# Corner additions of the gathered tiles: on TensorE in every stage but the context stage

## The reference, cut to what matters

```python
x = x + _L0_conv_ref(_gn(x), ...)   # focal modulation: projections, three depthwise convolutions, gating
x = x + _L1_conv_ref(_gn(x), ...)   # layer norm and a quantised gated MLP
x = x + _L2_conv_ref(_gn(x), ...)   # 7x7 convolutions by FFT, gates, scan, projection
x = x + _L3_conv_ref(_gn(x), ...)   # deformable convolution:

offsets = conv3x3(x, offset_w) + offset_b          # 2 numbers for each of 9 taps
py, px = pixel + tap + offsets;  y0, x0 = floor(py), floor(px);  wy, wx = py - y0, px - x0
val = gather(y0, x0)     * ((1 - wy) * (1 - wx)) + gather(y0, x0 + 1)     * ((1 - wy) * wx) \
    + gather(y0 + 1, x0) * (wy * (1 - wx))       + gather(y0 + 1, x0 + 1) * (wy * wx)
out = einsum('bhwkc,kcf->bhwf', val, kernel) + bias
```

## Time and profile before

| | |
|---|---|
| median of 3 runs | 5363.71 us (5361.05 to 5369.22) |
| profiled execution, its own time | 5375.03 us |
| its span, first to last instruction | 5373.1 us |
| mean granted clock of PE | 0.675 of full speed |
| PE busy | 3023.5 us (56%) |
| DVE busy | 3301.6 us (61%) |
| POOL busy | 2852.9 us (53%) |
| ACT busy | 1723.2 us (32%) |

### The profile page before, as it was taken

One profiled execution on the slowest core, in us unless ns is written; L12 is line 12 of the kernel. 1 busy time (PEld: TensorE's weight loads), 2 busy tenths in 40 slices (PEclk: granted clock), 3 DMA queues, 4 the chain that ended last, 5 costly groups with the idle time before them and its releaser, 6 DMA issues. The chain is left out here.

```text
span 5373.1 us, 93043 instructions
## 1 busy us (share of the span) xinstructions
PE 3023.5 (56%) x39604; PEld 2643.3 (49%) x39604; DVE 3301.6 (61%) x4084; ACT 1723.2 (32%) x3209; POOL 2852.9 (53%) x2614
## 2 busy tenths in 40 slices
PE   2873235669644466569644466579744563554333
PEld 2872135559533355469533365469633453543222
DVE  4357843575678755675688666666779655454333
ACT  1223424721333235522234246422333242240000
POOL 1000000365566655665565666665666766777776
PEclk9965655569767666759666676769666755665555
DMA  6541174568633575658523566659433657554333
GB/s 165 121 83 23 29 137 129 151 141 190 137 92 106 123 195 165 177 131 194 135 80 108 148 169 183 163 138 208 126 98 97 164 165 179 174 164 124 103 105 93
DMA packets 776762, 727.31 MB, mean 135 GB/s; under 512 B 575244, under 2 KB 677036, under 8 KB 771916
## 3 DMA queue, kind: packets, MB, share of 16 engines
q1 hardware_dynamic: 651931, 381.46, 30.9%
q0 software_dynamic: 124416, 339.90, 21.9%
HBM read 601.34 MB, written 136.73 MB: 137 GB/s over the span
## 5 line engine op out<-in xcount | busy, mean ns | idle before, releaser
L2146 POOL DMA_INDIRECT e_gb<-corner_table,e_idx x2592 | 2838.3, 1095 | 2500.8 <-DMA e_cws<-cw_all 1043.8
L2208 DVE TENSOR_TENSOR e_vw<-e_gb,e_pc 128x1024 f32<-128x1024 f32 x576 | 773.0, 1369 | 692.7 <-DMA e_gb<-corner_table,e_idx 671.8
L2174 PE MATMUL e_pv<-shifts,e_vw 128*128 128x128 f32 x2768 | 557.5, 373 | 390.8 <-DVE e_vw L2215 390.8
L2174 PEld LDWEIGHTS e_pv<-shifts,e_vw 128*128 128x128 f32 x2768 | 461.1, 195 | 424.6 <-DVE e_vw L2215 401.8
L488 PE MATMUL e_pw<-wk,e_vt 128*64 128x64 f32 (+1 forms) x2880 | 333.7, 290 | 447.2 <-DVE e_xr L2226 236.6
L488 PEld LDWEIGHTS e_pw<-wk,e_vt 128*64 128x64 f32 (+1 forms) x2880 | 287.1, 197 | 512.0 <-issue 269.8
L2184 ACT ACTIVATE e_vt<-e_pv 128x512 f32<-128x512 f32 x288 | 182.4, 633 | 791.8 <-PE e_pw L2174 783.3
L502 PE MATMUL b_p<-b_x,b_tt 100*100 100x96 f32 x4096 | 375.6, 251 | 2.0 <-ACT b_x L815 2.0
L502 PEld LDWEIGHTS b_p<-b_x,b_tt 100*100 100x100 f32 x4096 | 370.3, 169 | 2.4 <-issue 1.6
L489 PE MATMUL e_pw<-wk,e_vt 128*64 128x64 f32 (+1 forms) x2880 | 335.0, 291 | 0.0
L2215 DVE TENSOR_TENSOR e_vw<-e_vw 128x1152 f32<-128x1152 f32 x230 | 322.5, 1402 | 7.9
(11 more groups left out here) (310 smaller groups left out, 7125.6 us busy)
## 6 DMA issues: line engine op xcount, KB each, us to landing
e_gb<-corner_table,e_idx POOLq DMA_INDIRECT x2592
d_px<-x_halo SPq DMA_DIRECT2D x32, 1152.0 KB
corner_table<-f_xn SPq DMA_DIRECT2D x128, 288.0 KB
b_tt<-zl_copies SPq DMA_DIRECT2D x128, 273.0 KB
b_tt<-zl_copies SPq DMA_DIRECT2D x128, 195.0 KB
f_xall<-xpad SPq DMA_DIRECT2D x10, 2400.0 KB
x_halo<-d_xo SPq DMA_DIRECT2D x128, 144.0 KB
d_wd<-wd_rows SPq DMA_DIRECT2D x8, 1890.0 KB
```

The costliest lines, as they stand in the source:

```text
L2146: nc.gpsimd.indirect_dma_start(self.gb[k][:, 4 * q:4 * q + 4, :].rearrange("p a c -> p (a c)"), None, T.table[m], off)\
L2174: last = nc.tensor.matmul(dst, vw[:, a, 2 * q:2 * q + nq, :].rearrange("p k c -> p (k c)"), T.ident[:, :], start=(a == 0), stop=(a == n - ...
L2208: v.tensor_tensor(dst, self.gb[k][:, 4 * k0:4 * k1, :].rearrange("p (k a) c -> p k a c", a=4), bc(w, [128, k1 - k0, 4, C], 3), ALU.mult).t ...
```

## The change

One condition in `plan()` differs. A tile joins `whole` when it is placed in any stage but B, instead of in L alone.

```diff
@@ -2328,7 +2328,7 @@
         while tiles < J * loaded and due <= clock:
-            if s == 3:
+            if s != 1:
                 whole.add(tiles)
             tile(tiles)
             due += spaces[(tiles - 1) // (NI * J)]
```

## The result

The changed kernel takes 5334.44 us (median of 7 runs, 5320.75 to 5343.37) against 5366.17 for the one before, timed in the same rounds: a ratio of 0.9936, 95% interval 0.9925 to 0.9948, which is 34 us less (28 to 40). The forecast was no change. The time lies inside the stated range, but the likeliest case was wrong: the kernel is faster, by 0.6%, and that is clear of the noise.

A forecast was written before the change was run, and what follows sets the result against it. It took POOL's gathers to bound the last part and a chain changing engines before it. Transposes 51, additions -53, clock -15, neighbouring paths +13, turns joining the chain +4 summed to 0: 5364 us, range 5330 to 5398.

The forecast's parts named there:

- the likeliest case: Whole kernel: added transposes and dropped additions cancel, 5364 us, its own range 5353 to 5374, chance 0.37.
- What bounds the kernel.: POOL issuing 72 tiles' gathers paces the last 895.5 us; before that the chain changes engine every few us.
- Nearly all of their work is hidden by POOL's gathers.: POOL's part, 33 changed tiles: gathers cover nearly all of their work; priced at -2 to +4 us.
- 53 us at most: Additions dropped from DVE: 42 on the chain at 1.27 us each save 53 us at most, nothing at least.
- the quarter taken off it as lost: Where an addition leaves the chain, a neighbouring path may be nearly as long: 13 us of the saving lost.
- The count: Chain from 3133 to 4477 runs through 18 additions, so 40 over all three rounds before POOL's part.
- 37 sets at 1.39 us: Ten more transposes per changed tile on PE: 37 sets on the chain cost 51 us, ends 40 and 79.
- The credit: Longer bursts leave PE at the full clock for longer: 0.4 us a set, 37 sets, 15 us gained.
- the last rival: Transposes on PE don't raise the clock, every added ten cost 2.13 us: +43 us, 5407, chance 0.08.
- The copies' rival: ACT's copies wait for PE's turns, mainly in D and F, wait up over 60 us: +33, 5397, chance 0.21.
- The faster rival: Bursts carry PE's clock, all 53 us realised, turns cost 40, credit 22: -35 us, 5329, chance 0.34.

The follow-up runs named there:

- late33: Kernel before, with only the 33 changed tiles from tile 216 on switched to twenty transposes and no addition: ratio 0.9963, -20 us.
- early_psum: Kernel before, in 116 of the 130 changed tiles before tile 216 the addition replaced by a same-size DVE instruction with second input from PSUM: 0.9981, -10 us.
- tail39: Kernel before, with only the 39 last tiles, after all stages, switched to twenty transposes and no addition: ratio 0.9971, -16 us.
- pe_early: Kernel before, additions kept, twenty transposes with ten thrown away in only the 130 changed tiles before tile 216: ratio 1.0052, +28 us.
- pe_half: Kernel before, additions kept, twenty transposes with ten thrown away in all 163 changed tiles: ratio 1.0064, +34 us.
- dve_half: Kernel before, additions dropped in the 163 changed tiles without the ten more transposes, corners 2 and 3 left out: ratio 0.9857, -77 us.
- df: Kernel before, with only the 78 changed tiles before tile 216 in stages D and F switched: ratio 0.9991, -5 us.
- tail_sbuf: Changed kernel, 39 last tiles switched too, plus a DVE dummy with both inputs in SBUF in 34 of them: 0.9958, -23 us against the kernel before.
- tail_psum: Changed kernel, 39 last tiles switched too, plus a DVE dummy with second input from PSUM in 34 of them: 0.9912, -47 us against the kernel before.

## Why the prediction was wrong, step by step

**What bounds the kernel.** Right: POOL paces the part behind the last group's first gather, and before it the chain changes hands. That was the reason to look at what sets POOL's pace, and I stopped at "POOL issuing 72 tiles' gathers".

**"Nearly all of their work is hidden by POOL's gathers."** This step failed, and it alone moves the forecast out of its case. The 33 tiles were priced at -2 to +4 us in all and brought 20 (late33). The rule that idle or hidden work costs nothing was applied to an instruction that isn't neutral to the engine it hides behind. The rows were there in the trace of the kernel before: in the last part the gather that begins during each addition takes 1.39 us among eight of 0.95.

**What goes: "53 us at most".** Too small, and the quarter taken off it as lost was taken off for nothing. The DVE half measured 77 us against 53, and 40 realised. Without the last 33 tiles it is 57 to 71 against 51, and 38 realised. The hold-up, for which the sum has no term, is 3 to 18 of these (early_psum). The count itself is steady: the same stretch of the chain has 17 additions in late33 and in tail39, whose stages are the same, against 18. Whether an addition also costs the stages something that neither the chain nor the hold-up shows, no run here tells.

**What comes: 37 sets at 1.39 us.** Right for the half taken alone: +34 for all, +28 for the early ones, against 40 and 37. Behind the DVE half they cost 77 - 34 = 43 us for all and 71 - 13 = 58 for the early ones (57 - 13 = 44 by the other reading). The chain of the changed kernel, 3100 to 4445.3:

```profile
by line: PE b_p L502 8.6%; POOL e_gb L2146 8.4%; issue 7.4%; PE e_pv L2174 6.7%; DVE e_vw L2208 5.1%; ACT f_xall L1943 4.2%; PE d_p L495 3.0%; PE d_p L1550 2.9%; DMA e_gb<-corner_table,e_idx 2.6%; PE e_pw L488 2.4%; DVE gn_red L438 2.2%; DV
```

The turns of changed tiles are on it 25 times, against 15 before in as long a stretch. So a count in the kernel before misses sets that come onto the chain once they are longer. It doesn't tell why the halves don't add up: in pe_early and pe_half, which keep the additions, the turns are on the chain as often as in the changed kernel (from 3160 to tile 216's gather 34 pieces in both, against 33 there and 23 in the kernel before). Why is open. For the early tiles both terms were too small, the additions' by 19 to 33 us and the transposes' by some 7 to 21, and their difference, -13 against my 0, came out nearly right by luck.

**The clock.** The credit was right in kind. PE's other work takes 98 us less, 98/163 = 0.6 us for each changed tile; how much of it lies on the chain, which the forecast's 0.4 us a set was about, isn't shown. The mean clock rises to 0.710 in pe_half, which only adds transposes, and stays at 0.678 in dve_half, so it is the added transposes that raise it. Changed tiles' turns start slow and leave the clock up, as here in stage A, four us before, during and behind one:

```profile
3484.30:3488.30 4.00, 1.34 (x21) 1.26 (x22) 3.81 (x6) 0.00 (x0) 0.10 (x1) 0.50 0.00 0
3488.29:3492.30 4.01, 4.01 (x20) 3.90 (x20) 1.04 (x1) 0.00 (x0) 3.10 (x4) 0.50 0.20 65
3492.30:3496.30 4.00, 3.44 (x103) 3.07 (x102) 1.10 (x1) 1.78 (x6) 3.09 (x4) 0.99 0.41 116
```

The middle row holds most of the transposes of one tile and nothing else; PE had been busy for 1.34 of the 4 us before. The clock is at half speed through them and full behind them. This is the rule and not one case: of the 153 sets of twenty in the changed kernel that begin at the half clock, 134 end at the full one. Of the 177 sets of ten that begin so in the kernel before, 40 do. That settles the last rival: transposes do raise the clock here. The Trainium skill's sentence in "TensorE: Matmul & The Clock Gate", Part 4, that the full clock does not engage for them, is not borne out, and the measurement decides. (Of the 153 sets 33 took 4.4 us or more, so that nearly all of the set ran at the half clock.)

**The copies' rival.** ACT's wait for the turns went from 255.8 us to 297.5:

```profile
ACT e_vt L2184 <- PE e_pw L2174: 297.5, 66, 13.8
```

+42 us, not over 60, and switching the tiles of D and F cost nothing that can be measured (df: -11 to +2 us). The longer waits are there, but they don't show in the time.

**The faster rival** had the time almost to the us (5329 against 5334) by luck. It had -53 and +18 for the two halves, which measured -77 and +34, and it gave the 33 late tiles next to nothing.

## What to carry to other kernels

When an instruction is said to be hidden behind another engine's work, look at that engine's durations beside it: compare the same instruction with and without the neighbour, here 1.39 against 0.95 us. A DVE instruction with both inputs in SBUF is not free beside gathers that POOL issues, and it costs POOL what is left of it when the next gather is due. Take its second input from PSUM, or let PE's accumulation do it where PE has time. And in a chain that changes hands, measure the two halves of a swap apart as well as together: a total near the forecast can hide two wrong terms.

## What the runs showed of the hardware that was not expected

- The issue of an indirect gather by POOL takes 0.95 us. One that begins during a TENSOR_TENSOR of 1152 fp32 elements with both inputs in SBUF ends 0.82 us after that instruction, which made 1.39 and 1.48 us of it in the examples and 2.60 beside a stretched one. With the second input in PSUM it stays at 0.95 (tail_sbuf and tail_psum, 24 us apart).
- It is one-sided here: a gather already under way when the addition begins takes 0.95 us as well (130 of them in the kernel before), and the stretched additions of stage D are stretched with an input from PSUM too (early_psum, 2.43 us beside gathers of 0.95).
- Ten accumulating fp32 transposes of 128x128 more cost 1.09 us at the full clock and 2.13 at the half one, and they bring the clock up for what follows (134 of 153 sets of twenty that began at the half clock ended at the full one; 40 of 177 sets of ten).
